# Decoder layer on one core: the first layer norm folded into the second

## The reference, cut to what matters

```python
x = _layernorm(x + attention(x))                       # 16 heads, window of 128, rope, 4 batches of 256 tokens x 256
x = _layernorm(x + cross_attention(x, ctx))
x = _layernorm(x + moe(x))

def _layernorm(x, eps=1e-05):
    return (x - mean(x)) / sqrt(var(x) + eps)

def cross_attention(x, ctx):
    attention = softmax(query(ctx) @ key(ctx).T)       # 256 x 256 for a batch, no x in it
    return einsum('bln,bmn->blm', x, attention)
```

```
(r - m)/sqrt(v + eps) + (r A' - m)/sqrt(v + eps)  =  (w - 2 m)/sqrt(v + eps),   w = r + r A'
```

## Time and profile before

| what | us |
|---|---|
| three runs | 444.01, 452.41, 452.59 |
| median of them | 452.41 |
| the profiled execution: its time | 445.65 |
| its span, first to last instruction | 443.8 |
| mean granted clock of TensorE | 0.983 of full |
| batch period in the loop ("n" at 118.28, 178.60, 238.90) | 60.3 |

### The profile page before, as it was taken

One profiled execution on the slowest core, in us unless ns is written; L12 is line 12 of the kernel. 1 busy time (PEld: TensorE's weight loads), 2 busy tenths in 40 slices (PEclk: granted clock), 3 DMA queues, 4 the chain that ended last, 5 costly groups with the idle time before them and its releaser, 6 DMA issues.

```text
span 443.8 us, 8613 instructions
## 1 busy us (share of the span) xinstructions
PE 402.6 (91%) x2609; PEld 357.7 (81%) x2609; DVE 311.0 (70%) x865; ACT 256.7 (58%) x649; POOL 181.3 (41%) x314
## 2 busy tenths in 40 slices
PE   3976898999889999889998876999999999999994
PEld 2665687999778989779997765888999988899984
DVE  1596999797986888978979854457748535644444
ACT  3458977785657777456856542544636744444442
POOL 0044656554654464646536623374945500000000
PEclk9999999999999999999999988999989999999997
DMA  7611421000000000000000600792312312333211
GB/s 217 219 49 49 128 86 26 3 0 2 0 3 24 0 0 0 0 0 0 0 0 0 192 1 4 220 296 80 89 60 86 93 53 72 92 122 95 92 48 47
DMA packets 24359, 28.28 MB, mean 64 GB/s; under 512 B 2385, under 2 KB 16874, under 8 KB 24330
## 3 DMA queue, kind: packets, MB, share of 16 engines
q1 hardware_dynamic: 24330, 27.92, 20.5%
HBM read 26.80 MB, written 1.11 MB: 63 GB/s over the span
## 4 chain that ended last, share of the span: by engine, by line
PE 67%; DVE 14%; issue 7%; ACT 4%; DMA 3%; POOL 2%; SPq 1%; DVEq 0%; POOLq 0%; ACTq 0%
PE bank L630 18%; PE bank L631 17%; PE bank L632 17%; PE bank L747 4%; PE bank L756 3%; PE bank L746 2%; PE bank L719 2%; DMA gate_rows<-gates_d 2%; PE bank L819 1%; DVE by_cos L1207 1%; DVE by_sin L1208 1%; DVE pT_lo L1096 1%; PE bank L713 1%; DMA ctx_sb<-in_ctx 1%; DVE scores L1218 1%
## 5 line engine op out<-in xcount | busy, mean ns | idle before, releaser
L927 ACT ACTIVATE hid<-bank,b_cols 128x512 f32<-128x512 f32 (+1 forms) x50 | 34.4, 688 | 73.2 <-PE bank L632 60.4
L1109 DVE TENSOR_TENSOR hid<-hid,gate_rows 128x512 f32<-128x512 f32 (+2 forms) x46 | 33.4, 725 | 56.9 <-ACT hid L927 53.0
L1459 POOL TENSOR_SCALAR nprobs<-probs,rsums 128x128 f32<-128x128 f32 x64 | 24.2, 378 | 89.5 <-DVE rsums L1225 82.7
L631 PE MATMUL bank<-w_lo,hid_hi 128*128 128x256 f32 (+1 forms) x200 | 56.7, 283 | 0.0
L1451 POOL TENSOR_TENSOR queryT<-by_cos,by_sin 128x512 f32<-128x512 f32 x32 | 42.6, 1330 | 29.4 <-DVE by_sin L1208 28.4
L975 ACT COPY swapped<-bank 64x512 f32<-64x512 f32 x40 | 23.3, 583 | 31.9 <-PE bank L632 31.7
L1096 DVE TENSOR_TENSOR hid_lo<-hid,hid_hi 128x512 fp32r<-128x512 f32 (+1 forms) x50 | 37.0, 739 | 5.1 <-ACT hid_hi L939 4.9
L630 PE MATMUL bank<-xT_hi,wq_hi 128*128 128x256 f32 x128 | 38.4, 300 | 1.8 <-issue 1.2
L631 PEld LDWEIGHTS bank<-w_lo,hid_hi 128*128 128x128 f32 (+1 forms) x200 | 38.3, 191 | 2.0
L632 PE MATMUL bank<-x2T_hi,w_lo 128*128 128x512 f32 (+1 forms) x100 | 39.6, 396 | 0.0
L747 PE MATMUL bank<-keyT,queryT 128*128 128x256 f32 x128 | 38.7, 384 | 0.0
(11 more groups left out here) (174 smaller groups left out, 1287.1 us busy)
## 6 DMA issues: line engine op xcount, KB each, us to landing
gate_rows<-gates_d SPq DMA_DIRECT2D x16, 256.0 KB, 3.2
w_raw<-in_L_ffn_routed_w SPq DMA_DIRECT2D x4, 528.0 KB, 7.8
stage<-in_L_attn_q_kernel SPq DMA_DIRECT2D x4, 512.0 KB, 6.2
stage<-in_L_attn_out_kernel SPq DMA_DIRECT2D x4, 512.0 KB, 3.6
w_raw<-in_L_ffn_routed_w SPq DMA_DIRECT2D x2, 1024.0 KB, 9.1
gate_rows<-gates_d SPq DMA_DIRECT2D x8, 224.0 KB, 3.0
gate_rows<-gates_d SPq DMA_DIRECT2D x8, 192.0 KB, 2.8
gate_rows<-gates_d SPq DMA_DIRECT2D x8, 160.0 KB, 2.5
```

Of the source, the lines that this page charges most:

```text
L631: nc.tensor.matmul(o, sh, ml, start=False, stop=False, **kw)
L927: nc.scalar.activation(hid[0:n, i % 2, :], z_bank[i % 3][0:n, :], ACT.Relu, bias=b1_cols[0:n, i % NC:i % NC + 1]).then_inc(relu_done, 1)
L1109: nc.vector.tensor_tensor(hid[rows, i % 2, :], hid[rows, i % 2, :], gate_rows[rows, i % 3, :], ALU.mult).then_inc(gated, 1)
L1459: nc.gpsimd.tensor_scalar(nprobs[:, u, 0:W], probs[:, u, 0:W], rsums[:, u, 0:1], 1.0, ALU.mult, ALU.mult)
```

## The change

Raw residual rows go through n, m0 and m1; only then are they normed, once. `moments r` takes the residual's variance and turns it into eps (var + eps) and its -1/2; `moments w` takes the statistics of the sum and adds these. GpSimd does one Newton run a batch and then the scaling itself ("norm w"). "normed" on VectorE is gone. The late fills move 1.85 to 1.9 positions forward, which puts n between q5 and q6: ... v0, q5, n, q6, m0, m1, q7, y. In the last batch n follows step 0, m0 and m1 step 1, y step 5, ahead of `second_biases`; ScalarE splits two more steps of weights ahead of the loop, and GpSimd seven ahead of the norm.

```diff
--- before.py
+++ after.py
@@ -69,7 +69,7 @@
 
 SLOT_AT = {"x0": -2.5, "x1": -2.5, "q0": -1.25, "k0": -1, "q1": -0.75, "q2": -0.5, "q3": 1.75,
            "k1": 2.75, "q4": 4.75, "v1": 5.5, "v0": 6.5, "q5": 7.25, "q6": 7.75, "q7": 11,
-           "n": 25.5, "m0": 26.5, "m1": 26.75, "y": 29.25}
+           "n": 23.6, "m0": 24.6, "m1": 24.85, "y": 27.4}
 WINDOW = -2.5
 
 
@@ -100,12 +100,11 @@
            "out1": 11},
     "act": {"slot": 0, "exp": 0.75, "probs_hi": 3, "heads_hi0": 7.25, "heads_hi1": 9.25},
     "dve": {"slot": 0, "top": -0.5, "recip": 0.75, "probs_lo": 3, "heads_lo0": 7.25, "heads_lo1": 9,
-            "residual": 22.75, "moments 1": 23, "moments 2": 26.75, "normed 1": 24.25,
-            "normed 2": 27.5},
-    "pool": {"slot": 0, "normalise": 0.5, "norm 1": 22.75, "norm 2": 26.75, "keep": 28.75},
+            "residual": 22.75, "moments r": 24, "moments w": 24.8},
+    "pool": {"slot": 0, "normalise": 0.5, "norm w": 25.55, "keep": 27.5},
 }
 
-LATER = {"act": {"y": -0.25}, "dve": {"n": -0.5, "m0": -0.75, "m1": -0.25, "y": -0.25}}
+LATER = {"act": {"y": -0.25}, "dve": {"n": -0.2, "m0": -0.25, "m1": -0.1, "y": -0.25}}
 
 
 PIECE_NAMES = ["q0", "k", "q1", "q2", "v", "q3", "o0", "o1", "o2", "o3"]
@@ -277,10 +276,12 @@
         attT = sb("attT", [P, B, KC, T])
         xln = sb("xln", [P, TT, C])
         x1T = sb("x1T", [P, KC, T])
-        moments = sb("moments", [P, TT, 2])
+        moments = sb("moments", [P, 2, TT, 2])
         bn = sb("bn", [P, TT, 6])
         var_eps = sb("var_eps", [P, TT])
         half_neg = sb("half_neg", [P, TT])
+        eps_r = sb("eps_r", [P, TT])
+        half_eps_r = sb("half_eps_r", [P, TT])
         newton = sb("newton", [P, 2, TT])
         factor = sb("factor", [P, TT])
         unused = sb("unused", [P, 1])
@@ -405,7 +406,8 @@
         turned, pT_hi_done, pT_done = sem("turned"), sem("pT_hi_done"), sem("pT_done")
         pv_done, oT_hi_done, oT_done = sem("pv_done"), sem("oT_hi_done"), sem("oT_done")
         attn_done, res_done = sem("attn_done"), sem("res_done")
-        stats_done, aggr_done, moments_done = sem("stats_done"), sem("aggr_done"), sem("moments_done")
+        stats_done, aggr_done, eps_r_done, moments_done = (
+            sem("stats_done"), sem("aggr_done"), sem("eps_r_done"), sem("moments_done"))
         newton_done, ln_done, m_added = sem("newton_done"), sem("ln_done"), sem("m_added")
         kept, x2_hi_done = sem("kept"), sem("x2_hi_done")
         ld_ctx, ld_small, ld_w = sem("ld_ctx"), sem("ld_small"), [sem(f"ld_w{g}") for g in range(4)]
@@ -707,7 +709,10 @@
                     for t in range(TT):
                         mm = nc.tensor.transpose(o[:, t * P:(t + 1) * P], xb[:, t, j * P:(j + 1) * P], ident[:])
                 elif kind in "ny":
-                    e.wait_ge(ln_done, 2 * b + (1 if kind == "n" else 2))
+                    if kind == "n":
+                        e.wait_ge(res_done, b + 2)
+                    else:
+                        e.wait_ge(ln_done, b + 1)
                     for k in range(KC):
                         for t in range(TT):
                             mm = nc.tensor.transpose(o[:, k * T + t * P:k * T + (t + 1) * P],
@@ -884,17 +889,16 @@
                 if i + AFTER < NI:
                     up(i + AFTER)
                 down(i)
-                if i == 2:
+                if i == 0:
                     e.wait_ge(score_exp_done, 1)
                     e.wait_ge(gatesT_done, 1)
                     slot(z, "n")
-                if i == 4:
+                if i == 1:
                     slot(z, "m0")
                     slot(z, "m1")
                 if i == 5:
+                    slot(z, "y")
                     second_biases(0)
-                if i == 8:
-                    slot(z, "y")
                 if i == 10:
                     router(1)
                 if i == 16:
@@ -1068,15 +1072,17 @@
             hid_high(1)
             heads_hi(z, 3, 1)
             split(4)
+            split(5)
+            split(6)
 
 
             for i in range(2, NI):
                 relu(i)
                 if i > 2:
                     hid_high(i - 1)
-                if i + 3 < NC:
-                    split(i + 3)
-                if i == 11:
+                if i + 5 < NC:
+                    split(i + 5)
+                if i == 8:
                     slot(z, "y")
                 if i == 13:
                     score_exp(1)
@@ -1255,26 +1261,21 @@
                     ins = nc.vector.bn_stats(bn[:, t, :], xln[:, t, :])
                 ins.then_inc(stats_done, 1)
                 e.wait_ge(stats_done, m + 1)
-                if which or not (isinstance(b, int) and b == 0):
-                    e.wait_ge(ln_done, m)
+                if not (isinstance(b, int) and b == 0):
+                    e.wait_ge(ln_done, b)
                 e.sem_inc(dve_passed, 1)
                 for t in range(TT):
-                    ins = nc.vector.bn_aggr(moments[:, t, :], bn[:, t, :])
+                    ins = nc.vector.bn_aggr(moments[:, which, t, :], bn[:, t, :])
                 ins.then_inc(aggr_done, 1)
                 e.wait_ge(aggr_done, m + 1)
-                var = moments[:, :, 1:2].rearrange("p t a -> p (t a)")
-                nc.vector.tensor_scalar(var_eps[:], var, EPS, 1.0, ALU.add, ALU.mult)
-                nc.vector.tensor_scalar(half_neg[:], var, EPS, -0.5, ALU.add, ALU.mult).then_inc(moments_done, 1)
-
-            def normed(b, which):
-
-                m = 2 * b + which
-                e.wait_ge(newton_done, NEWTON_STEPS * (m + 1))
-                e.sem_inc(dve_passed, 1)
-                for t in range(TT):
-                    ins = nc.vector.tensor_scalar(xln[:, t, :], xln[:, t, :], moments[:, t, 0:1],
-                                                  newton[:, 0, t:t + 1], ALU.subtract, ALU.mult)
-                ins.then_inc(ln_done, 1)
+                var = moments[:, which, :, 1:2].rearrange("p t a -> p (t a)")
+                if which == 0:
+                    nc.vector.tensor_scalar(eps_r[:], var, EPS, EPS, ALU.add, ALU.mult)
+                    nc.vector.tensor_scalar(half_eps_r[:], var, EPS, -0.5 * EPS, ALU.add, ALU.mult).then_inc(eps_r_done, 1)
+                else:
+                    e.wait_ge(eps_r_done, b + 1)
+                    nc.vector.tensor_tensor(var_eps[:], var, eps_r[:], ALU.add)
+                    nc.vector.scalar_tensor_tensor(half_neg[:], var, -0.5, half_eps_r[:], ALU.mult, ALU.add).then_inc(moments_done, 1)
 
             n = [0]
 
@@ -1329,9 +1330,8 @@
                 e.sem_inc(s, 1)
             doers = {"slot": slot, "top": mask_and_top, "recip": recip, "probs_lo": probs_lo, "once": once,
                      "heads_lo0": lambda b, g: heads_lo(b, g, 0), "heads_lo1": lambda b, g: heads_lo(b, g, 1),
-                     "residual": residual, "moments 1": lambda b, _: moments_of(b, 0),
-                     "moments 2": lambda b, _: moments_of(b, 1),
-                     "normed 1": lambda b, _: normed(b, 0), "normed 2": lambda b, _: normed(b, 1)}
+                     "residual": residual, "moments r": lambda b, _: moments_of(b, 0),
+                     "moments w": lambda b, _: moments_of(b, 1)}
             step(nc.vector.memset(b1_rows[:], 0.0), "b1 cleared")
             nc.vector.memset(choice[:, :, NR:SC], NEVER)
             nc.vector.memset(gates[:], 1.0)
@@ -1397,7 +1397,6 @@
             hid_low(1)
             heads_lo(z, 3, 1)
             residual(z, 0)
-            moments_of(z, 0)
 
 
             for i in range(2, NI):
@@ -1406,17 +1405,14 @@
                     hid_low(i - 1)
                 if i in (3, 4):
                     twice(0, i - 3)
-                if i == 4:
-                    normed(z, 0)
-                if i == 5:
+                if i == 2:
                     slot(z, "n")
-                if i == 7:
+                    moments_of(z, 0)
+                if i == 3:
                     slot(z, "m0")
                     slot(z, "m1")
                     moments_of(z, 1)
-                if i == 9:
-                    normed(z, 1)
-                if i == 11:
+                if i == 8:
                     slot(z, "y")
                 if i == 14:
                     sigmoid(1)
@@ -1471,20 +1467,19 @@
 
             def keep(b, _):
 
-                e.wait_ge(ln_done, 2 * b + 2)
+                e.wait_ge(ln_done, b + 1)
                 e.sem_inc(pool_passed, 1)
                 nc.gpsimd.tensor_copy(res[:, bass.ds(b * TT, TT), :], xln[:]).then_inc(kept, 1)
 
-            def layer_norm(b, which):
-
-                m = 2 * b + which
+            def layer_norm(b, _):
+
                 done = [0]
 
                 def settled(ins):
                     done[0] += 1
                     ins.then_inc(newton_done, 1)
-                    e.wait_ge(newton_done, NEWTON_STEPS * m + done[0])
-                e.wait_ge(moments_done, m + 1)
```

(19 more changed lines are left out.)

## The result

| what | before | after |
|---|---|---|
| median | 448.3 (4 runs, 444.01 to 452.59) | 466.89 (4 runs, 466.57 to 471.61) |
| the profiled execution | 445.65 | 467.06 |
| its span | 443.8 | 465.2 |
| mean granted clock | 0.983 | 0.963 |

The ratio is 1.048, with a 95% interval of 1.041 to 1.055: slower, by 18.6 us on the medians and by 21.4 us on the two profiled spans. The forecast said +7.0. The sign was right, the size was not.

A forecast was written before the change was run, and what follows sets the result against it. TensorE, busy 91% of the span, was taken as the bound, its loop waits all at the norms. Loop +4.5 and last batch +2.5 made +7.0 us on the median 452.41: 459.4 us, own range 455 to 462, with rivals 446 to 467.

The forecast's parts named there:

- the two scalings: GpSimd's two scalings ahead of "y", priced at 0.48 us each from its one-column scaling of 128x256.
- wait before "y": TensorE in each loop batch asks for "y" at 126.85, gets it at 130.2: a wait of 3.4 us, before 1.5.
- waits on "twice": In the last batch TensorE waits 2.1 and 2.0 us for VectorE's additions of twice the residual, behind moments.
- last residual to end: The last batch's feed-forward stretch: waits of 4.1 us instead of 1.24, a loss of +2.5 us.
- The bank step: With "n" between q5 and q6, q6 waits 1.1 us for q5's bank and m1 0.6 for q6's.
- The queue step: Moments are ready at 122.3, but GpSimd's queue holds the Newton run behind normalise 9 until 125.25.
- "n" and "x0": TensorE's waits before these fills in the loop go, gaining 0.9 and 0.5 us per batch.
- rival D: Each GpSimd scaling takes 1.56 us, "y" 2.2 us later each time: +13.6 us, 466.0; chance 0.10.
- rival A: Clock falls in the loop's new waits, up to 1.7 us lost each time: +12, 464.5; chance 0.20.
- three batches: The loop's loss of 1.5 us per batch was counted three times, +4.5 us in all.
- the split edits: Weight splits of ScalarE and GpSimd moved ahead of loop and norm were said to cost nothing.

The follow-up runs named there:

- experiment 7: Changed kernel with GpSimd's scaling reduced to a multiplication by one column, the mean not subtracted: 462.65 us.
- experiment 4: Changed kernel with the norm's two scalings given back to VectorE, all else as changed: 462.04 us.
- experiment 3: Changed kernel with 36 unread transposes on TensorE ahead of its wait for "y" in the loop: 461.92 us.
- experiment 5: Kernel before with only the fold (raw rows, one Newton run a batch), old places, scaling on VectorE: 442.32 us, 0.986 of before.
- experiments 11: The kernel of experiment 5 with "n" at 25 instead of 25.5, nothing else: 440.06 us, 0.983 of the kernel before.
- experiment 12: Kernel before with the fold in its old places, "n" at 25, two Newton steps instead of three: 438.34 us, 0.979 of before.
- experiment 6: Changed kernel with VectorE's moments in the last batch moved behind the "twice" of the same step: 469.03 us.
- experiment 9: Changed kernel with "y" at its old place and GpSimd's norm behind normalise 10: 461.53 us, one run.
- experiment 2: Changed kernel with "n" behind q6 in the fills and its VectorE copy behind q6's multiplications: 467.17 us.

## Why the prediction was right in sign and wrong in size

The first turn of the changed kernel, its times less 2.75 (what its first residual came late), beside the steps of the prediction:

| step | predicted | measured |
|---|---|---|
| q6 starts | 112.7, wait 1.1 | 112.67, wait 0.92 |
| wait before m1 | 0.6 | 0.61 |
| TensorE asks for "y" | 126.85 | 127.28 |
| Newton run starts | 125.25 | 125.91 |
| the run, to the scaling | 3.95 | 3.84 |
| the two scalings | 0.96 | 2.43 |
| wait before "y" | 3.4 | 5.05 |
| clock | 1.00 | 0.50 behind "y" |
| waits on "twice" | 2.1 and 2.0 | 1.96 and 1.82 |
| last residual to end | +2.5 | +2.2 |

**Right.** The bank step: q6 behind "n" waits for q5's cosine, and m1 for q6's. The queue step: the moments are ready, but normalise 9 stands ahead of the run and VectorE's masks and copies ahead of its reciprocal. "n" and "x0" no longer wait. The two waits on "twice", each within 0.2.

**Wrong, first: the price of the scaling.** The text took "0.48 each", from the one-column scaling of the earlier trace rows, and gave the 1.56 of rival D a chance of 0.10. It is 1.22 in the form with two columns (experiment 7). The two instructions make 1.5 of the 1.7 by which the wait at "y" came out too long, and experiment 4 gives back 5.1 us with the scaling on VectorE.

**Wrong, second: the clock was a rival and not a term.** The text stood at a wait of 3.4, below the 3.68 of the earlier trace rows, and gave rival A 0.20. The wait was 5.05, and the granted clock went to the lower level of 1.2 GHz at each turn. Rival A's price, at most 1.7 a turn, was a little low: 5.9 us in all by the spans of experiment 3, 7.1 by its three turns. That price rests on 3.4 us of work at half speed, of which the earlier trace rows shows one; the trace of the kernel before has the clock below 1.00 from 272.1 to 275.5, so the length was near, but the changed kernel has it so from 134.3 to 141.1 and from 199.1 to 206.0 in its first two turns, about twice as long. The two errors hang together, since the dear scaling lengthened the wait. But experiment 4 shows that a wait of 3.3, the size I had forecast, brings the clock down too: with the wait as forecast, A held. The Trainium skill, TensorE: Matmul & The Clock Gate, section "HAM oscillation", describes such a loop, where each turn starts again at the low clock; the trace agrees, with three dips at three equal distances. I had cited it and let one row outweigh it.

**Wrong, third, and in part only: the first batch.** The text counted "three batches" of late work. But the order of the banks counts the places of all fills, also in the first batch, where the late ones are absent. There q6 sits in q5's bank with nothing between them, and waits 2.03 at 57.78. Most of that wait is absorbed before the first residual (idle time +0.30). What stays is clock, 2.45 us, and it falls in two places. One lies right behind the wait, from 59 to 63 us (the window from 60 to 62 shows 0.50). Such a fall, between 57 and 64, is in six of the eight kernels with "n" ahead of q6 and in none of the six with the old order, so I put it down to the change, though it doesn't come each time. The other lies from 39 to 42. It needs no change: experiments 5 and 11 keep the old order, have it too (0.86 and 0.85 between 40 and 55 us), and reach their first residual at 111.71 and 112.06, while the kernel before and experiment 12 don't have it. So 2.75 is no clean price of the change; the runs leave open how much of it is.

**The last batch came out right by two misses.** The waits there grew by 3.7, not 2.5: the "twice" waits were as forecast, but the split edits, costed at nothing, added 1.1 (w_lo in the waits). Against that, the clock of this part was 0.98 in the profile before and 0.99 after, which gives 1.4 back and has nothing to do with the change that I can show: the busy time of this part is 148.09 and 149.71 in experiments 11 and 12, which have the same orders there.

**The sum again.** Idle time: 0.3 + 3 x 3.4 + 3.7 = 14.1, of which the prediction had 7.0; the later "y" is 3 x 1.7 = 5.1 of what is missing, the splits 1.1, the rest 0.9. Clock: 2.4 + 6.3 - 1.4 = 7.3, of which the sum had none; the 6.3 of the loop are the change's by experiment 3, the other two terms in part or not at all. Together 21.4.

## What to carry to other kernels

A change that removes work and moves work is two changes. Here the removal was worth 1.4% (experiment 5), and the moves with the scaling on GpSimd lost some 6% (span 465.2 against 440.2); one kernel with every place left as it was shows it. Before a wait is shortened, look at what stands behind the moved work in its queue: three times here (turn 10, m0, split 8) a wait that was taken away came back one place further on. And a wait that repeats in a loop is priced with the clock behind it, half as much again in this case (6.3 us on 10.1 of waits in the loop), once it comes near to any wait after which the trace shows the lower level.

## What the runs showed of the hardware that I had not expected

GpSimd's multiplication of 128x256 by one column takes 0.48 us, and its subtraction of one column with a multiplication by another 1.22 (experiment 7, eight instructions each). Beside the feed-forward part, in experiment 6, the pair took 3.34.

VectorE's own scaling has two durations. In the kernel before it starts at 130.09, in the same moment as GpSimd's addition of the rotated queries, and the pair takes 1.74. In experiment 4 GpSimd does only small parts of normalise 10 beside it, and the pair takes 0.79. The line's instructions, before and in experiment 4 (min/median/max ns):

```profile
L1275 DVE TENSOR_SCALAR xln<-xln,moments,newton x16: 401/818/1441, 116.4 to 314.2; 128x256 f32<-128x256 f32 x16
```

```profile
L1284 DVE TENSOR_SCALAR xln<-xln,moments,newton x8: 407/412/465, 132.5 to 317.8; 128x256 f32<-128x256 f32 x8
```

So 1.74 was a price with company. That the addition is what stretches it is read from these two traces; no kernel here moved it alone.

The clock falls behind shorter waits than the 3.68 of the earlier trace rows, and not always at once. It fell behind waits of 3.30 to 3.32 in all three turns of experiment 4, and behind 3.50 to 3.52 in all three of experiment 7. In the first of these the transposes of "y" still ran at the full clock, and it fell just behind them:

```profile
133.45 0.63 PE L718 MATMUL bank<-ident,xln 128*128 128x128 f32 x4 [3.52 <-POOL xln L1498]
```

```profile
197.13 1.09 PE L718 MATMUL bank<-ident,xln 128*128 128x128 f32 x4 [3.50 <-POOL xln L1498]
```

```profile
133.00:139.00 6.00, 5.55 (x25) 4.76 (x26) 3.88 (x16) 3.67 (x12) 3.74 (x7) 0.72 0.00 1
197.00:201.00 4.00, 3.87 (x15) 3.51 (x16) 1.82 (x6) 2.32 (x7) 2.02 (x3) 0.50 0.00 0
```

There the clock is down from 134.4 to 137.8, in the second turn from 195.9 to 202.7, and the turns are 63.65 and 64.73 long. So the length of the first matmuls behind a wait does not tell whether the clock has fallen; a window of some microseconds does. Shorter waits go either way: it fell behind 2.6 in the first two turns of experiment 9, and behind the 2.84 before m0 in the second turn of experiment 2, but not behind the same wait in the first. Behind 1.45 it stayed up in the first two turns of experiment 5. What decides between turns with the same wait no run here shows.
